# Value-weight products moved in the preparation, two swaps in the turn and one more wait on GpSimd in a slot-attention and expert kernel

## What is computed

```python
Pn = rmsnorm(P, input_norm_w)
k_proj = Pn @ Wk.T
v_proj = Pn @ Wv.T
for _ in range(NUM_ITERS):                       # 3
    sn = rmsnorm(slots, slot_norm_w)
    scores = einsum('bkd,bmd->bkm', sn @ Wq.T, k_proj) * SCALE
    attn = softmax(scores, axis=-2)              # over the 1024 slots
    attn = attn / (sum(attn, axis=-1) + EPS)     # over the 64 context tokens
    updates = einsum('bkm,bmd->bkd', attn, v_proj)
    slots = gru_cell(updates, slots, ...)
...
x = x + tanh(g_xattn) * slots_out
x = x + tanh(g_ffn) * ffn(layernorm(x))
```

## Time and profile before

| | |
|---|---|
| median of 3 runs | 1107.53 us (1107.29 to 1108.12) |
| the profiled execution | 1108.25 us, its span 1106.5 us |
| TensorE, matmuls | 1079.6 us busy, 98% of the span |
| VectorE | 778.8 us, 70% |
| ScalarE | 546.2 us, 49% |
| GpSimd | 341.7 us, 31% |
| mean granted clock of TensorE | 0.994 |

### The profile page before, as it was taken

One profiled execution on the slowest core, in us unless ns is written; L12 is line 12 of the kernel. 1 busy time (PEld: TensorE's weight loads), 2 busy tenths in 40 slices (PEclk: granted clock), 3 DMA queues, 4 the chain that ended last, 5 costly groups with the idle time before them and its releaser, 6 DMA issues.

```text
span 1106.5 us, 17708 instructions
## 1 busy us (share of the span) xinstructions
PE 1079.6 (98%) x6087; PEld 930.8 (84%) x6087; DVE 778.8 (70%) x1504; ACT 546.2 (49%) x830; POOL 341.7 (31%) x352
## 2 busy tenths in 40 slices
PE   6899999999999999999999999999999999999996
PEld 4687888888888778888888888988889888888896
DVE  7888687878789877787556666566665666656663
ACT  4455545454447843333555554455454544545442
POOL 6123444444205100000214233343333433324332
PEclk9899999999999999999999999999999999999999
DMA  7601010101226441212663443544434445344421
GB/s 247 153 1 34 6 38 1 39 1 39 79 78 192 149 129 20 38 20 40 194 192 94 134 115 119 148 99 130 132 104 147 107 125 144 92 143 123 111 35 20
DMA packets 61323, 105.39 MB, mean 95 GB/s; under 512 B 12128, under 2 KB 50272, under 8 KB 56928
## 3 DMA queue, kind: packets, MB, share of 16 engines
q1 hardware_dynamic: 43904, 82.78, 23.4%
q0 software_dynamic: 16512, 21.50, 12.0%
q10 hardware_dynamic: 864, 0.55, 0.2%
HBM read 74.11 MB, written 21.27 MB: 86 GB/s over the span
## 4 chain that ended last, share of the span: by engine, by line
PE 92%; DVE 5%; issue 1%; DMA 1%; ACT 1%; POOL 0%; SPq 0%; DVEq 0%
PE wide L1313 30%; PE wide L867 16%; PE down L1327 16%; PE wide L1162 8%; PE down L1174 4%; PE down L935 3%; PE wide L874 3%; PE wide L876 3%; PE wide L1359 2%; PE side L1299 1%; PE side L1146 1%; PE side L305 1%; PE side L959 1%; PE down L1373 1%; DVE stats L1896 1%
## 5 line engine op out<-in xcount | busy, mean ns | idle before, releaser
L2310 DVE SCALAR_TENSOR_TENSOR hid<-wide,b_up,silu 128x512 f32<-128x512 f32 x120 | 90.1, 751 | 161.4 <-PE wide L1313 154.9
L1313 PE MATMUL wide<-xt_hi,w_hi 128*128 128x512 f32 x480 | 188.4, 392 | 0.0
L1313 PE MATMUL wide<-xt_lo,w_hi 128*128 128x512 f32 x480 | 187.8, 391 | 0.0
L1313 PE MATMUL wide<-xt_hi,w_lo 128*128 128x512 f32 x480 | 186.9, 389 | 0.0
L838 POOL DMA_INDIRECT out_tokens<-y,idx_out x64 | 111.4, 1741 | 220.1 <-DVE y L2291 175.0
L1690 ACT ACTIVATE silu<-wide,b_gate 128x512 f32<-128x512 f32 x120 | 82.1, 684 | 143.7 <-PE wide L1313 143.7
L1327 PE MATMUL down<-w_hi,hid_hi 128*128 128x256 f32 x480 | 136.5, 284 | 0.0
L1327 PE MATMUL down<-w_lo,hid_hi 128*128 128x256 f32 x480 | 135.7, 283 | 0.0
L1327 PE MATMUL down<-w_hi,hid_lo 128*128 128x256 f32 x480 | 135.7, 283 | 0.0
L1699 ACT ACTIVATE hid_hi<-hid 128x512 fp32r<-128x512 f32 x120 | 76.0, 633 | 100.2 <-DVE hid L2310 100.2
L2261 DVE TENSOR_TENSOR w_lo<-raw,w_hi 128x768 fp32r<-128x768 f32 x128 | 121.4, 949 | 2.5 <-ACT w_hi L1664 2.5
(11 more groups left out here) (329 smaller groups left out, 2266.9 us busy)
## 6 DMA issues: line engine op xcount, KB each, us to landing
raw<-in_w_expert SPq DMA_DIRECT2D x32, 1536.0 KB, 6.8
x_raw<-in_x SPq DMA_DIRECT2D x16, 256.0 KB, 6.8
out_tokens<-slots SPq DMA_DIRECT2D x16, 256.0 KB, 3.8
token_rows<-work SPq DMA_DIRECT2D x8, 512.0 KB, 3.0
out_tokens<-y POOLq DMA_DIRECT2D x8, 512.0 KB, 6.0
attn<-rms_c SPq DMA_DIRECT2D x24, 128.0 KB, 2.3
attn<-expo SPq DMA_DIRECT2D x22, 128.0 KB, 2.3
x_first<-in_x SPq DMA_DIRECT2D x8, 256.0 KB, 3.2
```

What stands on the lines that cost most here:

```text
L1313: last = nc.tensor.matmul(bank[:, f % 2, :], w[f // HALF_F][:, f % HALF_F, (c + k) * P:(c + k + 1) * P], x_[:, k, :], start=(m == 1), stop ...
L2310: nc.vector.scalar_tensor_tensor(hid[:, f % 2, :], eup[:, f % 2, :], b_up[:, bass.ds(e, 1), f:f + 1].rearrange("p a b -> p (a b)"), silu[: ...
```

## The change

It moves the value weights. Block 1 goes from ahead of the transposes to behind `spread_rms(0, 0)`, block 2 ahead of the column sums, block 3 behind them, into the bank of the gate x. On ScalarE the high parts of groups 1 and 3 go ahead of the first `copy_rms`, block 1's copy behind the second, and the exponentials ahead of the copies of blocks 2 and 3. On TensorE the second `spread_rms` goes between the two halves of the scores. In the turn the subtraction of group 0 goes ahead of the transposes of group 4, and the transposes of group 5 go ahead of `turn_h(2)`. On GpSimd the squares of group 2 in the first iteration get one more wait, for the reciprocals of the second softmax.

```diff
@@ -381,8 +381,8 @@
-            small_banks = (side[:, 1, :], down[:, 0, :], down[:, 1, :], side[:, 0, :])
-            vw_bank = (1, 2, 3, 0)
+            small_banks = (side[:, 1, :], down[:, 0, :], down[:, 1, :], side[:, 0, :], gate_x)
+            vw_bank = (1, 3, 3, 4)
...
@@ -732,6 +732,8 @@
                         pool.wait_ge(s_ss, run - 1)
+                        if run == G + 2:
+                            pool.wait_ge(v_recd, 2)
                         multiply(g)
...
@@ -1076,26 +1078,25 @@
                 value_weights(0)
-                value_weights(1)
                 pe.wait_ge(e_w, 3)
                 turn_rms(0)
                 turn_first(1)
                 turn_first(3)
                 spread_rms(0, 0)
-                value_weights(2)
-                spread_rms(0, 1)
+                value_weights(1)
                 pe.wait_ge(a_whi, B)
                 pe.wait_ge(p_wlo, B)
-                pe.wait_ge(e_w, 5)
+                pe.wait_ge(e_w, 4)
                 scores(0, 0, (2, 4), True, (0,))
+                spread_rms(0, 1)
                 scores(0, 0, (2, 4), True, (1,))
-                pe.wait_ge(a_rms, 2)
-                value_weights(3)
                 pe.sem_inc(s_ss, G)
                 pe.wait_ge(p_wlo, B + 2)
                 gru_unit(0, 0, 0, 0, None, ("first",))
-                pe.wait_ge(e_w, 7)
+                pe.wait_ge(e_w, 5)
+                value_weights(2)
                 column_sums(0)
+                value_weights(3)
                 turn_rec(0)
...
@@ -1209,14 +1210,14 @@
                 def turn_and_subtract():
+                    subtract_hi(0)
                     turn_slots(4, (v_x1, 2))
-                    subtract_hi(0)
 
                 gru_unit(LAST, 1, 1, 1, turn_and_subtract)
                 turn_h(1, (a_hlo, 1))
                 gru_unit(LAST, 1, 2, 0, lambda: subtract_hi(1))
+                turn_slots(5, (v_x1, 5))
                 turn_h(2, (a_hlo, 2))
-                turn_slots(5, (v_x1, 5))
                 gru_unit(LAST, 1, 2, 1, lambda: subtract_hi(2))
...
@@ -1549,15 +1550,15 @@
                 value_weights(0)
-                value_weights(1)
-                copy_rms(0, 0, True)
                 first_high(1)
                 first_high(3)
+                copy_rms(0, 0, True)
                 copy_rms(0, 1, True)
+                value_weights(1)
                 own_weights(0)
+                exponentials(0)
                 value_weights(2)
                 value_weights(3)
-                exponentials(0)
                 own_weights(1)
```

## The result

| | before | after |
|---|---|---|
| median | 1107.87 us (5 runs, 1107.29 to 1108.36) | 1114.1 us (5 runs, 1111.6 to 1114.8) |
| profiled execution | 1108.25 us, span 1106.5 | 1113.04 us, span 1111.3 |
| granted clock, mean | 0.994 | 0.993 |

The ratio is 1.0054, 95% interval 1.0041 to 1.0067: slower, by 6.2 us between the medians, where I had forecast +1.4 and a range up to 1111.5. The profiled execution is one of the quicker ones after the change, 4.8 us over the one before; what follows decomposes those 4.8 us first.

A forecast was written before the change was run, and what follows sets the result against it. TensorE, busy 98% of the span, was taken as the bound. Terms 0 + 0.6 - 0.5 + 1.3 = +1.4 us on the median 1107.53 gave 1108.9 us, with a range from 1107.0 to 1111.5.

The forecast's parts named there:

- The clock after the wait: TensorE idle 4 us before the first attention product; lower clock behind it costs 0 to 1.1 us, taken as +0.6.
- the turn: Two swaps on TensorE: a 0.43 us later VectorE start plus 0.87 us of lost cover, +1.3 us, bounds 0.9 and 1.5.
- A: Slower rival, chance 0.22: long clock fall after the attention wait, 47.6 to 54.3 us, losing 2.8 us; total 1111.1 us.
- B: Slower rival, chance 0.10: clock falls in the turn for 3.3 us from 367, costing 1.7 us; total 1110.6 us.
- the held pass: GpSimd's squares of group 2 near 96 us wait for VectorE's reciprocals: -0.5 us, bounds -0.69 and 0.
- The preparation, up to the exponentials: Earlier rounding of high parts brings VectorE's low parts, scores and softmax forward: column sums 0.6 us earlier, bounds 0 and 0.9.
- What holds the gain back: GpSimd's subtraction and SyncE's queue before the attention: first product 0.4 us later, mostly absorbed by a later wait; together 0.

The follow-up runs named there:

- slots5_alone: Kernel before with one swap of the turn alone, the transposes of group 5 ahead of turn_h(2): 1108.47 us, ratio 1.0013.
- prep_alone: Kernel before with only the preparation's part of the change; held GpSimd pass and turn as before: 1111.79 us, ratio 1.0037.
- high_spread_hold: Kernel before with early high parts of groups 1 and 3, second spread_rms between the scores' halves, and GpSimd's extra wait: 1106.94 us, ratio 1.0000.
- hold_alone: Kernel before with GpSimd's one extra wait alone: 1107.09 us, ratio 0.9997.
- prep_queue: prep_alone with SyncE's transfers of the second pair's high value weights moved behind the first attention's: 1110.61 us, ratio 1.0024 to the kernel before.
- turn_swap1: Kernel before with the turn's other swap alone, subtraction of group 0 ahead of the transposes of group 4: 1108.28 us, ratio 1.0006.
- prep_early_att: prep_queue with GpSimd's second subtraction held behind the attention's low parts, and small VectorE instructions moved behind attention work: 1109.64 us, ratio 1.0014.

## Why the prediction was wrong

**What failed** is the step "The clock after the wait", and the turn's sum, which had no clock in it. I took +0.6 between 0 and 1.1 for the first and nothing for the second, put the long falls into A and B, and let them stand as alternatives to the forecast and to each other. Both came in the same execution. A gave 1.2 GHz from 47.6 to 54.3 us and 2.8 us lost; the profile has 47.5 to about 54.2, and A-C is +1.88, or 2.3 with the 0.43 us wait that it also swallowed. B gave 3.3 us at 1.2 GHz and 1.7 us lost; it was some 3.4 us and 1.60. With both, my own terms come to 2.8 - 0.5 + 1.3 + 1.7 = +5.3: 1113.6 us counted from the profiled execution before, beside 1113.04 measured, and 1112.8 from the median, beside 1114.1. Against the terms of my sum the legs say: the preparation +2.94 (W-S, S-A and A-C) where I had 0 + 0.6, the held pass -0.52 where I had -0.5, the turn +2.97 (R-5 and 5-6) where I had +1.3. My arguments against A (dense products soon bring the clock back) and against B (dense products ran before the wait) were both beside the point: the low stretches lasted as long as those that I had before me, and full work up to 363.0 did not prevent one.

The Trainium skill, TensorE: Matmul & The Clock Gate, under "What's actually happening", says that the gate's timing runs free of the kernel, so that one kernel meets it at another moment in each execution. The runs agree: slots5_alone, one program, has nine runs within 1.8 us and three about 3 us higher at a lower mean clock, and behind the same idle piece of 1.97 us at 22 us the clock fell in prep_alone and not in after. A range worked out from one profile of before, as mine was, misses that.

**The preparation, up to the exponentials**: 0.6 us earlier was too much. W-S is 0.34 us shorter than the 17.06 at full clock; high_spread_hold says 0.25. VectorE's own two copies held its low parts to some 0.2 us (they start 7.36 us behind W after, 7.58 in hold_alone). It also misses the idle piece that the moved block left, 1.97 us at 22 us, which cost 1.67 us in prep_alone.

**What holds the gain back**: both mechanisms are in the rows. half_b_hn took 1.36 us and SyncE's transfers started at 42.06 (42.5 forecast). The first product at 48.73 looks like a hit on 48.7, but by luck: W came 0.69 us early. From W on it is 28.25 us against 27.19, so +1.06 and not +0.4. S-A grew by 1.57: 0.70 until ScalarE's transfers are issued (45.47 less 37.20, against 45.97 less 38.40), which the 0.6 of the column sums was to cover, and 0.87 from there to the product (3.26 against 2.39 us), where I had 0.34. What makes the latter stays open: prep_queue, without the 786 KB in front, has the same 3.26 us, and so has slots5_alone, whose preparation is that of before, while the nine others with that order have 2.38 to 2.54.

**The held pass**, -0.5: the leg says -0.52, the cast took 0.18 us, TensorE's wait 0.17, the square ran 99.38 to 101.28 and the product beside it 2.22 us. **The turn**, +1.3 without the clock: 0.47 and 0.89. Both right, though one reading behind the first was not. VectorE does not work without a pause from 353 to 365 us; before, its timeline has

```profile
361.42 1.23 DVE L1742 TENSOR_TENSOR dif<-slots,nn 128x1024 f32<-128x1024 f32 x1 [0.79 <-ACT nn L1421]
```

The delay came through all the same, 0.45 us in turn_swap1.

**From +4.8 to +6.2.** The profiled execution after had no fall at 24 us and an early W. prep_alone, prep_queue and prep_early_att had that fall. With 1.67 us for it in part of the executions and 0.7 us for W the median is within reach, but the share of executions was not measured. The mean clock was 0.993 in the profiled execution and 0.990 to 0.992 in the other four; but the quickest of all, 1111.6 us, is one of these four, so this stays argued.

## What to carry to other kernels

Work that is moved out of a wait, or from ahead of one, is not free even if the wait is as long as before: it had kept TensorE busy. Price a lengthened idle piece ahead of dense work on the path at its own length and, in part of the executions, 1.6 to 2.3 us of lower clock besides; the runs here give no length below which it is safe (it fell behind 1.50 us in one profile and not behind 1.97 in another). Where several lengthen, count them together and not as alternatives. Cut one timeline at fixed instructions and compare legs, and look first how far a leg repeats in kernels that leave it alone: C-R told 0.5 us in five kernels, where medians of eleven runs could not tell 0.6.

## What the runs showed that I had not expected

The low stretches that began between 16 and 60 us or between 350 and 380 us lasted about 3.4 or 6.8 us (once 10.2) in all seventeen profiles, and the idle piece ahead of one does not decide it alone: behind 1.97 us of idleness at 22 us the clock fell in prep_alone and not in after. A low clock can also be harmless. Before, it lay at 41 to 47.6 us ahead of a wait that hid it; after, that stretch was at full clock, and the next one, on the path, was low.

GpSimd's passes of 1.8 us held the small VectorE instruction that came first behind their start: half_b_hn for 1.36 us, or half_b_rz for 1.61. The Trainium skill, SBUF — State Buffer, under "Who interferes with whom", says that a tensor_scalar can, in its two-port modes, take the ports that VectorE shares with GpSimd, and that whichever comes second is blocked for the whole of the other; the rows agree, down to two elements a row: half_b_hn ended at 43.98, the pass at 43.95. Holding the pass only chooses its victim, so it pays where the victim has slack: at 99 us, and not at 45.
